# Zero rows stored from ScalarE's queue in 2 KB pieces, seven sequences in the first half, and a re-laid order

## The reference, cut to what matters

```
x = block0(x, ctx)   # pre-norm: causal self attention, cross attention, relu feed-forward (1024)
x = block1(x, ctx)   # post-norm: causal self attention, cross attention,
                     #   then a mixture of 8 experts: every token goes to its top 2
    combine[t, top2] = softmax(top2 of softmax(x @ router_w + router_b))
    h  = gelu(x @ w1[e] + b1[e]);  eo = h @ w2[e] + b2[e]
    x  = ln(x + sum_e combine[t, e] * eo[e, t])
x = block2(x, ctx)   # post-norm: masked self attention, cross attention, relu feed-forward
x = block3(x, ctx)   # one cross attention, residual, layer norm
```

## Time and profile before

| | us |
|---|---|
| median of 3 runs | 3278.52 |
| lowest, highest | 3277.52, 3300.14 |
| the profiled execution | 3263.0 |
| its span | 3261.2 |
| PE busy in the span | 3031.6 (93%) |
| DVE, ACT, POOL busy | 1574.7, 1548.4, 871.0 |
| PE's mean granted clock | 0.96 |

### The profile page before, as it was taken

The page is one execution under the profiler, slowest core; times in us unless marked ns, Lnnn a source line. Parts: engine busy times, 40 slices in busy tenths (PEclk is TensorE's granted clock), DMA queues, the critical chain, the costliest instruction groups (busy, mean ns, idle before and its releaser), DMA issues. The chain is left out here.

```text
span 3261.2 us, 61820 instructions
## 1 busy us (share of the span) xinstructions
PE 3031.6 (93%) x23913; PEld 2467.9 (76%) x24016; DVE 1574.7 (48%) x4057; ACT 1548.4 (47%) x3403; POOL 871.0 (27%) x991
## 2 busy tenths in 40 slices
PE   7899999999999999885999999889999999999996
PEld 5788877788887788663888888656777777777774
DVE  4544556655466656353101011166555666666552
ACT  4555555564655656352222222145556555665552
POOL 3112224232223423222000000152233343433241
PEclk8999999899999999995999999989999999999997
DMA  9635446535445743832666666374425564556231
GB/s 169 95 54 67 63 54 99 81 65 70 78 59 73 108 59 70 186 49 96 235 220 222 198 204 202 101 118 64 60 49 75 77 85 62 78 76 78 39 57 26
DMA packets 394607, 319.34 MB, mean 98 GB/s; under 512 B 151711, under 2 KB 378271, under 8 KB 394303
## 3 DMA queue, kind: packets, MB, share of 16 engines
q1 hardware_dynamic: 371062, 276.77, 47.1%
q0 software_dynamic: 8272, 23.73, 3.1%
q10 hardware_dynamic: 14981, 14.89, 1.6%
HBM read 134.33 MB, written 37.22 MB: 53 GB/s over the span
## 5 line engine op out<-in xcount | busy, mean ns | idle before, releaser
L1085 DVE TENSOR_REDUCE a_maxima<-a_bank 128x2 f32<-128x512 f32 (+3 forms) x576 | 340.1, 646 | 136.8 <-PE a_bank L706 136.2
L936 ACT ACTIVATE a_prob<-a_bank 128x512 f32<-128x512 f32 (+1 forms) x640 | 338.1, 599 | 121.3 <-PE a_bank L726 114.9
L936 ACT ACTIVATE c_prob<-c_bank 128x512 f32<-128x512 f32 (+1 forms) x512 | 263.7, 599 | 142.5 <-PE c_bank L726 140.8
L972 ACT ACTIVATE b_group_hidden<-b_bank,b_b 128x256 f32<-128x256 f32 x312 | 131.0, 471 | 421.3 <-PE b_bank L794 421.3
L1085 DVE TENSOR_REDUCE c_maxima<-c_bank 128x2 f32<-128x512 f32 (+2 forms) x448 | 266.3, 638 | 93.1 <-PE c_bank L706 91.8
L839 PE MATMUL a_bank<-a_causal_b,keep_identb 128*128 128x256 bf16 (+1 forms) x768 | 246.2, 321 | 43.0 <-DMA a_qs<-a_shift 25.5
L794 PE MATMUL b_bank<-b_group_xt,b_w 128*128 128x256 f32 x1248 | 284.0, 381 | 0.8 <-DVE b_group_xt L1126 0.8
L778 PE MATMUL b_bank<-b_w,b_group_hidden 128*128 128x256 f32 x1248 | 275.8, 379 | 0.9 <-ACT b_group_hidden L972 0.9
L778 PEld LDWEIGHTS b_bank<-b_w,b_group_hidden 128*128 128x128 f32 x1248 | 237.0, 190 | 33.5 <-ACT b_group_hidden L972 1.3
L794 PEld LDWEIGHTS b_bank<-b_group_xt,b_w 128*128 128x128 f32 x1248 | 235.5, 191 | 31.9 <-DVE b_group_xt L1126 1.2
L1131 DVE TENSOR_TENSOR b_group_y<-b_bank,b_b 128x512 f32<-128x512 f32 x39 | 27.0, 691 | 364.4 <-PE b_bank L778 364.4
(11 more groups left out here) (239 smaller groups left out, 6496.2 us busy)
## 6 DMA issues: line engine op xcount, KB each, us to landing
b_w<-in_L_xattn_e_w SPq DMA_DIRECT2D x78, 1024.0 KB, 7.1
a_qs<-a_parts_q SPq DMA_DIRECT2D x384, 128.0 KB, 4.4
c_qs<-c_parts_q SPq DMA_DIRECT2D x288, 128.0 KB, 4.3
a_ks<-a_parts_k SPq DMA_DIRECT2D x192, 128.0 KB
c_ks<-c_parts_k SPq DMA_DIRECT2D x96, 128.0 KB
b_group_x<-sorted_in SPq DMA_DIRECT2D x39, 256.0 KB, 6.6
sorted_out<-b_group_y ACTq DMA_DIRECT2D x39, 256.0 KB, 4.8
sorted_in<-a_zeros SPq DMA_DIRECT2D x8, 1024.0 KB, 10.4
```

Source lines behind the costliest of these rows:

```text
L936: act.activation(prob[0:rows, first:first + cols], bank[0:rows, 0, 0:cols], ACT.Exp, scale=SCALE).then_inc(k.own(s), 1)
L972: ins = act.activation(hidden[:, f, :], bank[:, 0, j * S:(j + 1) * S], ACT.Gelu, bias=b1[:, f:f + 1])
L1085: v.tensor_reduce(maxima[:, q:q + qn, h:h + n].rearrange("p q h -> p h q"), bank[:, 0, 0:cols].rearrange("p (j q n) -> p j q n", j=n, q=qn ...
```

## The change

1. **The zero stores.** The tile `zeros` is 512 wide, so a piece is 2 KB, with two rows of `sorted_in`; each partition writes neighbouring rows. ScalarE issues them. The eight stores at counted places still follow `clear_from`; the ninth (`clear_past`), at a fixed place, is issued near the start, as soon as `fold` is done and `zeros` is filled.
2. **Seven lanes** in the first half instead of six, eight `tok` buffers instead of seven, and one `loaded` buffer instead of two.
3. **Split weights.** Of the first cross attention's four matrices the k and v ones (`"1c"`) are loaded early, the q and o ones after the first `shift_in`. The context steps wait for `"1c"` alone.
4. The load of the constant ones at the start of phase c is issued by ScalarE; the estimate of a `gather` is 1.25 for 0.95.
5. `AHEAD` has other entries in both halves, so that the list of every engine is another one in phases a and c. Phase b's lists are the same, step for step.

```diff
-LANES = {"a": 6, "c": 7}
+LANES = {"a": 7, "c": 7}
...
-         "bias": ("scalar", None), 1: ("sync", ("enter", 1, "a")), "rows": ("sync", ("enter", 2, "a")), "gains": ("sync", ("shift_in", 0, 1)),
+         "bias": ("scalar", None), "1c": ("sync", ("enter", 1, "a")), 1: ("sync", ("shift_in", 0, 0)), "rows": ("sync", ("enter", 2, "a")), "gains": ("sync", ("shift_in", 0, 1)),
...
+    plan.step("vector", "zeros", -1, "a", us=0.3, after=[("fold", -1, "a")])
+    plan.step("scalar", "clear_past", -1, "a", us=0.5, lag=15.0, after=[("zeros", -1, "a")], takes=["zeros"], landing="zeros",
+              zeros=("zeros", "a"))
...
-        plan.step("vector", "clear_from", b, "a", us=0.4, after=[("run", b, "a"), ("fold", -1, "a")])
-        for e in range(E + 1):
-            plan.step("sync", "clear", b, "a", e, us=1.3, lag=6.0, after=[("clear_from", b, "a")], behind=[("clear", b, "a", e - 1)] if e else [],
-                      takes=["zeros"] if e == 0 else [], landing="zeros", zeros=("zeros", "a"))
+        plan.step("vector", "clear_from", b, "a", us=0.2, after=[("run", b, "a")])
+        for e in range(E):
+            plan.step("scalar", "clear", b, "a", e, us=1.3, lag=10.0, after=[("clear_from", b, "a"), ("clear_past", -1, "a")],
+                      behind=[("clear", b, "a", e - 1)] if e else [], landing="zeros", zeros=("zeros", "a"))
...
-    plan.step("sync", "load", -1, "c", "ones", us=2.0, lag=2.0, takes=["w"], landing="w", transfers=len(loads["c", "ones"]),
+    plan.step("scalar", "load", -1, "c", "ones", us=2.0, lag=2.0, takes=["w"], landing="w", transfers=len(loads["c", "ones"]),
...
+def zero_rows(k, rows, n):
+
+    return (k.sorted_in[rows, :].rearrange("(p q k) d -> p q (k d)", p=P, k=2),
+            k.zeros.unsqueeze(1).broadcast_to([P, n // (2 * P), 2 * D]))
...
+        elif s.kind == "clear_past":
+            until.wait_ge(*done("zeros", -1, "a"))
+            act.dma_start(*zero_rows(k, slice(E * REGION, ROWS_SORTED), (E - 1) * GROUP)).then_inc(k.own(s), 16)
+        elif s.kind == "clear":
+            until.wait_ge(*done("zeros", -1, "a"))
+            until.wait_ge(*done("clear_from", b, "a"))
+            first = act.value_load(k.clear_from[0:1, s.part:s.part + 1], min_val=0, max_val=E * REGION - ROWS_CLEARED)
+            act.dma_start(*zero_rows(k, bass.ds(first, ROWS_CLEARED), ROWS_CLEARED)).then_inc(k.own(s), 16)
...
-        elif s.kind == "clear":
-            rows = lambda first, n: (k.sorted_in[first, :].rearrange("(q p) d -> p q d", p=P),
-                                     k.zeros.unsqueeze(1).broadcast_to([P, n // P, D]))
-            until.wait_ge(*done("clear_from", b, "a"))
...
-    pool("tok", 7 if name == "a" else 8, [P, QT, D])
-    pool("loaded", 2, [P, QT, D])
+    pool("tok", 8, [P, QT, D])
+    pool("loaded", 1 if name == "a" else 2, [P, QT, D])
...
+        if at == 1:
+            c.loads["1c"] = c.loads[1][1:3]
+            del c.loads[1][1:3]
...
-    k.zeros = c.sb("zeros", [P, D])
+    k.zeros = c.sb("zeros", [P, 2 * D])
```

More of the change, by code:

```diff
@@ L274, in parts_steps @@
     stack = ({"q": "qs", "k": "ks", "c": "ctx_ks"}[role], (b, at))
-    plan.step("tensor", "proj", b, at, role, us=0.9 if role == "c" else 1.73, source=source, after=list(after) + weights_in(plan, at),
+    plan.step("tensor", "proj", b, at, role, us=0.9 if role == "c" else 1.73, source=source, after=list(after) + weights_in(plan, at, role == "c"),
               takes=["bank", "parts", "stack"], gives=gives, xt=xt, bank=bank, parts=parts, stack=stack)
@@ L294, in value_steps @@
     bank, values = ("bank", ("vals",) + lab), ("ctx_values" if role == "cv" else "values", (b, at))
-    plan.step("tensor", "value_proj", b, at, us=1.73 * f, source=source, after=list(after) + weights_in(plan, at), takes=["bank", "values"], gives=gives,
+    plan.step("tensor", "value_proj", b, at, us=1.73 * f, source=source, after=list(after) + weights_in(plan, at, role == "cv"), takes=["bank", "values"], gives=gives,
               xt=xt, bank=bank, values=values)
@@ L453, in ahead_of, with weights_in @@
     return lambda s: (by.get(STAGE_OF.get(s.kind), 0.0) + by.get((STAGE_OF.get(s.kind), NORM_OF.get(s.at, s.at)), 0.0))
-def weights_in(plan, at):
-    key = ("load", -1, "a", at)
+def weights_in(plan, at, context=False):
+    key = ("load", -1, "a", "1c" if at == 1 and context else at)
     return [key] if key in plan.steps else []
@@ L576, in second_half @@
     for j in range(2 * QT):
-        plan.step("gpsimd", "gather", b, "c", j, us=0.95, lag=4.0, behind=[("gather", b, "c", j - 1)] if j else [("enter", b, "c")],
+        plan.step("gpsimd", "gather", b, "c", j, us=1.25, lag=4.0, behind=[("gather", b, "c", j - 1)] if j else [("enter", b, "c")],
                   takes=["y"] if j == 0 else [], landing="y", y=y)
@@ L660, in tensor_program @@
         b, at = s.b, s.at
-        for weights in weights_in(k.plan, at):
+        for weights in weights_in(k.plan, at, at in CROSS and (s.kind == "value_proj" or s.part == "c")):
             until.wait_ge(*done(*weights))
@@ L1033, in vector_program @@
             ins.then_inc(k.own(s), 1)
+        elif s.kind == "zeros":
+            until.wait_ge(*done("fold", -1, "a"))
+            v.memset(k.zeros, 0.0).then_inc(k.own(s), 1)
         elif s.kind == "clear_from":
             until.wait_ge(*done("run", b, "a"))
-            until.wait_ge(*done("fold", -1, "a"))
-            v.memset(k.zeros, 0.0)
             v.tensor_copy(k.clear_from, k.run[0:1, CLEAR_AFTER, :]).then_inc(k.own(s), 1)
@@ L1308, in gpsimd_program @@
             if b >= CLEAR_AFTER:
-                until.wait_ge(*done("clear", CLEAR_AFTER - 1, "a", E))
+                until.wait_ge(*done("clear", CLEAR_AFTER - 1, "a", E - 1))
             for t in range(QT):
@@ L1350, in sync_program @@
             sp.dma_start(tile(s, "qs")[STACK:STACK + NPART, :, :], tile(s, "shift")).then_inc(k.own(s), 16)
-        elif s.kind == "clear":
-            rows = lambda first, n: (k.sorted_in[first, :].rearrange("(q p) d -> p q d", p=P),
-                                     k.zeros.unsqueeze(1).broadcast_to([P, n // P, D]))
-            until.wait_ge(*done("clear_from", b, "a"))
-            if s.part < E:
-                first = sp.value_load(k.clear_from[0:1, s.part:s.part + 1], min_val=0, max_val=E * REGION - ROWS_CLEARED)
-                dst, src = rows(bass.ds(first, ROWS_CLEARED), ROWS_CLEARED)
-            else:
-                dst, src = rows(slice(E * REGION, ROWS_SORTED), (E - 1) * GROUP)
-            sp.dma_start(dst, src).then_inc(k.own(s), 16)
         elif s.kind == "x1_store":
```

35 lines of the change are left out of this document (20 added, 15 removed).

## The result

| | before | changed |
|---|---|---|
| median, 20 runs each | 3284.78 us | 3300.89 us |
| lowest, highest | 3270.11, 3300.14 | 3294.51, 3313.18 |
| span of the profiled execution | 3261.2 | 3307.3 |

The ratio of the changed kernel to the one before is 1.005, 95% interval 1.0038 to 1.0062: 16 us slower, where the forecast was 26 us faster. The time lies outside the range of 3224 to 3290. By the forecast's own bound of 1% the case is "within 1%", its likeliest class, but on the wrong side, and the sum had one term wrong by 50 us.

A forecast was written before the change was run, and what follows sets the result against it. TensorE was taken to set the pace, leaving its idle and half-clock time to win. Terms -12 + 1 - 2 - 10 - 3 = -26 us gave 3252.5 us for the median (3278.5); range 3224 to 3290.

The forecast's parts named there:

- Phase c's order: Phase c, 2165 to 3200 us: the new order wins 3 us of 29.0 idle, bounds 12 either way.
- rival 1: New order is neutral, only the stores' place and the start count: -13 us, 3265.5; chance 0.20.
- if phase c moved by more than 12 us: Sign named in advance that the forecast is wrong: phase c's time changes by over 12 us.
- The stores, -12 forecast: Zero stores leave SyncE: 16.3 us of shift wait and slow clock go, 4 come back from full engines; 12 won.
- rival 2: Shift and copies wait all the same because the 16 DMA engines are full: -19 us, 3259.5; chance 0.12.
- Rival 3: Store issues hold ScalarE, sequence 13's shift waits behind seven stores: +22 us, 3300; chance 0.11.
- The ninth store, +1: Early store near 150 us meets the weight loads there: 1 us lost, bounds 0 and 5.
- Start, -2: Start: early "1c" and context load win 5.3 us, the single `loaded` buffer loses 3.3; 2 won.
- Seven lanes and the order, -10: 200 to 1340 us: 67.7 us idle or half clock, about a seventh less; 10 won, bounds 34 won, 20 lost.
- Phase b 0: Phase b keeps its lists: no change.
- ones on ScalarE 0: Phase c's start: SyncE's other loads start 2.3 us sooner, but VectorE's first mix waits for a gather: 0, bound 2.3 won.
- the tail of phase a 0: Last stretch of phase a, 65 us idle, keeps its 129 last steps on TensorE: no change.

The follow-up runs named there:

- c_ctx_act: Changed kernel, all lists kept, but in phase c five of six context copies issued by ScalarE instead of SyncE: ratio to the kernel before 1.0099, phase c 1215.1 us.
- ctx_lag: Changed kernel with the estimated landing of a context copy in phase c raised from 2.4 to 6.0 us: ratio to the kernel before 0.9951.
- a_unsplit: a_new_c_old with the four matrices of the first cross attention in one load again: ratio to the kernel before 0.99.
- a_new_c_old: Changed kernel's phase a with phase c of the kernel before (its table, gather estimate, ones on SyncE): ratio to the kernel before 0.9902, phase c 1157.8 us.
- c_ctx_act_old: a_new_c_old, all lists kept, but in phase c five of six context copies issued by ScalarE: ratio to the kernel before 1.0038, phase c 1195.0 us.

## Why the prediction was wrong, point by point

**The step that failed: "*Phase c's order*: 29.0 us idle at stake, bounds 12 either way, 3 us won."** It measured +47 us. Two errors are in it. The first is that of the bound: the idle time at hand limits what a new order can win, but not what it can lose, and I set the same bound on both sides. The second is the thought in rival 1, "estimates laid this order as they laid the last". Eight other orders, laid by the same rules with the old or the new numbers mixed or one of them changed, took 1181 to 1205 us; at 1152 to 1160 the old one isn't one sample among equals, but the best of ten. A new draw was far likelier to lose than to win, and the profile of before said so: 195 to 196 of 200 us busy at a clock of 1.00, the best stretch of the kernel, with nothing to win in it. I read this as safety. The prediction's own last sign of being wrong, "if phase c moved by more than 12 us", came true.

**What makes it slow** is shown down to this: the order of phase c alone costs it, by TensorE's waits, the largest of them for context copies that come late, and the clock lost behind them, 27 and 20 us in 600. That bunched projections make the copies late is read from two traces and was not isolated, since the one edit that should have done it, c_ctx_act, held up ScalarE. Nor was it separated whether they wait more in SyncE's queue or at the full DMA engines, and ctx_lag shows a bunched order that hardly waits. This stays open.

**The stores, -12 forecast:** -15 (0.9953) alone, in a list laid anew, and -4 in the new order. The mechanism was half right. The wait of 14.4 us went, as forecast, no wait for `a_shift` over 4 us stands there, and ScalarE's issues take 0.557 us at the median (0.4 to 0.9 forecast). But another came, 8.44 us, with the clock at 0.50 behind it, most likely for copies of q and k: rival 2, the full engines, is partly true. Two thirds of the 15 us came without ScalarE's queue. Rival 3 gave 3300 us, the time that was measured, but by luck: ScalarE was not held, as its 0.557 us show.

**The ninth store, +1:** not separated. It lands in 13.4 us, and where it does, the engines are full with TensorE at 0.50 as before; but it did less in these 5 us:

```profile
160.00:165.00 5.00, 4.33 (x12) 3.50 (x13) 0.00 (x0) 3.49 (x7) 0.00 (x0) 0.50 1.06 402
```

**Start, -2:** nothing that can be told from the spread of executions. GpSimd's `bias` stands at 11.79 (near 14 forecast), the second transpose at 23.01 (after 22), but the context wait didn't go: 3.67 for 5.34 us. Idle to 200 us: 33.8 for 31.7, but 31.1 to 36.9 in twelve executions of the changed lists and 36.5 in a second one of the old. a_unsplit shows no gain of the split either.

**Seven lanes and the order, -10:** all of phase a gave -32 by a_new_c_old, stores included; less 4 to 15 for the stores, 17 to 28 remain. The direction and the idle time (38.6, forecast 35 to 40) were right, the size was taken too small. The traces don't show all of it: idle time fell by 6 to 14 us there, by which of the two traces of the old lists one takes. That a table and the number of lanes hold only together was not seen.

**Phase b 0, ones on ScalarE 0, the tail of phase a 0**: right. Phase b lasts 572 us in both traces, and in the last 130 us ahead of it TensorE is idle 47.9 us before and 48.4 after.

The forecast sum was -23 for phase a with the start, measured -32; -3 for phase c, measured +44 to +47. Had phase c been kept, 3285 x 0.9902 = 3253 would have been the time. That this is the forecast's 3252.5 is luck: the median of before was taken 6 us too low (3278.5 for 3284.8), and the gain 6 us too small (26 for 32).

## What to carry to other kernels

Read a re-laid order as a new draw, and price it by how good the old one is: the idle time there bounds the gain, nothing in the profile bounds the loss. Where a stretch is 98% busy at full clock, keep its order and change the rest; here that version is 1.5% faster than the whole change (0.9902 against 1.005). In a new order look first at the one queue that all copies share: how many transfers stand in a row in it, and which one that is needed soon stands behind them. In this kernel that was a mark of slow orders, not a proven cause.

## What the runs showed of the hardware

- Issues of 0.64 us between ScalarE's activations, 160 in 1200 us on an engine that is 56% busy there, cost 1.4% of the kernel (c_ctx_act_old, 0.9902 to 1.0038): a queue on a computing engine is not free, though no share of busy time says so.
- With the same lists, phase b begins anywhere within some 15 us from one execution to the next, on several chips (1537 and 1552 us with the old lists, 1513 to 1529 with the new), so terms of this size can't be read from one pair of traces.
- Copies of 128 and 38.5 KB in small pieces hold the 16 DMA engines at a share of 1.19 (118 GB/s) to 1.40 (94 GB/s) in the changed kernel from 2592 to 2604 us; zeros in 2 KB pieces reach 373 to 402 GB/s at 1.06 to 1.07. A full DMA share says nothing of the bandwidth.
